# Gram products of the nodes divided between the first and the second layer's loop of the edge MLP

## The reference

```python
edge_index = jnp.stack([src, dst])
x = _layernorm(x + _L0_gnn_ref(src, dst, x, edge_attr_3, ...), axis=-1)   # attention on edges
x = _layernorm(x + _L1_gnn_ref(x, ..., edge_index), axis=-1)              # mean + batch norm
x = _layernorm(x + _L2_gnn_ref(x, src, dst, ...), axis=-1)
x = _layernorm(x + _L3_gnn_ref(x, edge_index, ...), axis=-1)

# in _L0_gnn_ref: an MLP on the three attributes of every edge
d = jax.nn.gelu(layer_norm(x @ Wd1 + bd1, g1, b1), approximate=False)
d = jax.nn.gelu(layer_norm(d @ Wd2 + bd2, g2, b2), approximate=False)
# in _L1_gnn_ref: statistics of h over all nodes
mu = jnp.mean(h, axis=0)
var = jnp.mean(jnp.square(h - mu), axis=0)
```

## Time and profile before

| | us |
|---|---|
| median of three timed runs | 4470.37 (4461.03 to 4475.22) |
| the profiled execution | 4428.03 |
| its span, first to last instruction | 4426.2 |
| GpSimd's scatter L482, first to last start | 162.2 to 485.4 |
| GpSimd's gather L497, first to last start | 489.9 to 786.7 |

### The profile page before, as it was taken

The page is one execution under the profiler, slowest core; times in us unless marked ns, Lnnn a source line. Parts: engine busy times, 40 slices in busy tenths (PEclk is TensorE's granted clock), DMA queues, the critical chain, the costliest instruction groups (busy, mean ns, idle before and its releaser), DMA issues. The chain is left out here.

```text
span 4426.2 us, 57341 instructions
## 1 busy us (share of the span) xinstructions
PE 2895.4 (65%) x14794; PEld 2110.8 (48%) x14794; DVE 2552.0 (58%) x4677; ACT 1648.0 (37%) x3762; POOL 2222.2 (50%) x2199
## 2 busy tenths in 40 slices
PE   0356782233433566998999999996879889942332
PEld 0255551122222455765666666664657655532221
DVE  3687741488888543454788877776633322233343
ACT  0233332133333000665788777871112133321111
POOL 0477777778777575001772000000057666567777
PEclk9976655566666666998999999996766699955555
DMA  3465302122222233566321111113455544422221
GB/s 106 121 153 133 89 0 60 43 61 65 59 58 61 65 79 70 121 132 136 85 62 59 57 57 57 57 49 70 92 122 147 140 126 126 114 67 50 51 56 33
DMA packets 879648, 364.12 MB, mean 82 GB/s; under 512 B 641845, under 2 KB 821447, under 8 KB 879570
## 3 DMA queue, kind: packets, MB, share of 16 engines
q1 hardware_dynamic: 815582, 335.56, 29.9%
q0 software_dynamic: 64000, 27.78, 3.3%
HBM read 237.51 MB, written 157.11 MB: 89 GB/s over the span
## 5 line engine op out<-in xcount | busy, mean ns | idle before, releaser
L1167 POOL DMA_INDIRECT g_W<-d,pos x400 | 422.0, 1055 | 1081.8 <-DMA g_W<-s 966.9
L859 POOL DMA_INDIRECT at_W<-in_x,at_idx x400 | 478.7, 1197 | 127.1 <-issue 125.4
L2788 POOL DMA_INDIRECT rows<-d,pos x200 | 212.0, 1060 | 408.8 <-DMA rows<-s 346.6
L919 PE MATMUL at_pA<-ident,at_W 128*128 128x128 f32 x200 | 55.7, 433 | 452.9 <-DMA at_W<-in_x,at_idx 413.0
L2641 PE MATMUL ou_pA<-ident,ou_W 128*128 128x128 f32 x200 | 55.1, 431 | 347.1 <-DMA ou_W<-d,pos 345.4
L482 POOL DMA_INDIRECT where<-mg_stage_v,mg_stage_i x200 | 243.2, 1216 | 71.2 <-issue 55.1
L919 PEld LDWEIGHTS at_pA<-ident,at_W 128*128 128x128 f32 x200 | 35.7, 216 | 466.0 <-DMA at_W<-in_x,at_idx 374.9
L1167 POOL DMA_INDIRECT me_W<-d,pos x200 | 207.6, 1038 | 99.3 <-issue 60.7
L1167 POOL DMA_INDIRECT ou_W<-d,pos x200 | 202.2, 1011 | 91.5 <-issue 60.7
L588 PE MATMUL mg_pG<-mg_z 128*128 128x129 f32 (+1 forms) x784 | 152.3, 372 | 142.2 <-DVE mg_z L729 142.2
L497 POOL DMA_INDIRECT mg_stage_v<-where,mg_stage_i x200 | 205.8, 1029 | 71.8 <-issue 55.0
(11 more groups left out here) (457 smaller groups left out, 8509.3 us busy)
## 6 DMA issues: line engine op xcount, KB each, us to landing
de_X<-x SPq DMA_DIRECT2D x98, 256.0 KB
out<-de_O SPq DMA_DIRECT2D x98, 256.0 KB, 2.2
mg_x<-in_x SPq DMA_DIRECT2D x97, 256.0 KB
x<-mg_z SPq DMA_DIRECT2D x97, 256.0 KB, 4.0
ix_win<-in_dstp SPq DMA_DIRECT2D x50, 256.5 KB, 3.2
at_V<-mlp SPq DMA_DIRECT2D x100, 128.0 KB
s<-g_HS SPq DMA_DIRECT2D x50, 256.0 KB
d<-g_HD SPq DMA_DIRECT2D x50, 256.0 KB, 2.3
```

Of the source, the lines that this page charges most:

```text
L859: gp.indirect_dma_start(out=W[w][b][:, (2 * t + h) * C:(2 * t + h + 1) * C], out_offset=None, in_=a["x"], in_offset=bass.IndirectOffsetOnAxis(
L919: i = t.transpose(pA[b][:, n * P:n * P + P], W[w][b][:, n * P:n * P + P], k.ident[:, :])
L1167: nc.gpsimd.indirect_dma_start(out=slot(w, b, t), out_offset=None, in_=table, in_offset=bass.IndirectOffsetOnAxis(ap=k.pos[:, c:c + 1], ax ...
L2788: nc.gpsimd.indirect_dma_start(out=k.rows[:, c * C:c * C + C], out_offset=None, in_=k.d2, in_offset=bass.IndirectOffsetOnAxis(ap=k.pos[:, ...
```

## The change

The first loop now has 25 iterations of one pair step and one edge part each, in which TensorE has the first layer ahead of the products of the pair before. The last iteration of it leaves one pair centred but not scaled. The third loop has, in each of its 25 iterations, the gelu part as before and one further pair step (the last one only finishes pair 48): 24 pairs are begun there. ScalarE now loads gelu's table set and the Ln and Exp set in turn, once each for an iteration. The loops of SP, ScalarE and VectorE that were loops of the hardware with registers as addresses are written out in the first and third loop. GpSimd's program and the second loop are not changed.

```diff
--- before.py
+++ after.py
@@ -446,7 +446,7 @@
         d = {n: g.sem("d_" + n) for n in ("sum", "cen", "sq", "sumsq", "ln", "dev", "norm", "gram")}
         pairs = D_FULL // 2 + 1
         ones_z = g.sem("ones_z")
-        assert D_FULL % 2 == 1 and pairs % 2 == 1 and pairs // 2 + 1 == ITERS
+        assert D_FULL % 2 == 1 and pairs % 2 == 1 and pairs == 2 * ITERS - 1
 
         def sizes(q):
             return (P, D_REST) if isinstance(q, int) and q == pairs - 1 else (P, P)
@@ -524,15 +524,15 @@
                         .then_inc(attr_in, 16)
                 load(0, 0)
                 load(1, 1)
-                with sp.Fori(0, pairs // 2 - 1) as j:
-                    load(2 * j + 2, 0)
-                    store(2 * j, 0)
-                    load(2 * j + 3, 1)
-                    store(2 * j + 1, 1)
-                load(pairs - 1, 0)
-                for q in range(pairs - 3, pairs):
-                    store(q, q % 2)
-                with sp.Fori(0, ITERS) as j:
+                for q in range(ITERS):
+                    load(q + 2, q % 2)
+                    if q:
+                        store(q - 1, 1 - q % 2)
+                for j in range(ITERS):
+                    q = ITERS + j
+                    if q + 2 < pairs:
+                        load(q + 2, q % 2)
+                    store(q - 1, 1 - q % 2)
                     for b in range(2):
                         sp.wait_ge(e["gelu", 2], last_of(j, b))
                         rows = k.mlp[:, bass.ds((2 * j + b) * CE, CE)].rearrange("c (n h e) -> c n h e", h=2, e=P)
@@ -589,15 +589,10 @@
                         i.then_inc(d["gram"], 1)
 
                 pe.wait_ge(attr_in, 64)
-                first_layer(0)
-                gram(0, 0)
-                for j in range(pairs // 2 - 1):
-                    gram(2 * j + 1, 1)
-                    first_layer(j + 1)
-                    gram(2 * j + 2, 0)
-                gram(pairs - 2, 1)
-                first_layer(ITERS - 1)
-                gram(pairs - 1, 0)
+                for j in range(ITERS):
+                    first_layer(j)
+                    if j:
+                        gram(j - 1, 1 - j % 2)
                 for b in range(2):
                     turn(0, b, 1)
                 with pe.Fori(0, ITERS - 1) as j:
@@ -607,9 +602,10 @@
                         turn(j + 1, b, 1)
                 for b in range(2):
                     second_layer(ITERS - 1, b)
-                with pe.Fori(0, ITERS) as j:
+                for j in range(ITERS):
                     for b in range(2):
                         turn(j, b, 2)
+                    gram(ITERS - 1 + j, j % 2)
 
             @block.scalar
             def _(act_):
@@ -654,15 +650,9 @@
                         square_edges(j, b, 1)
 
                 s.preload_act_table_set(LN_EXP)
-                deviate(0, 0)
-                squares(0)
-                with act_.Fori(0, pairs // 2 - 1) as j:
-                    deviate(2 * j + 1, 1)
-                    deviate(2 * j + 2, 0)
-                    squares(j + 1)
-                deviate(pairs - 2, 1)
-                deviate(pairs - 1, 0)
-                squares(ITERS - 1)
+                for j in range(ITERS):
+                    deviate(j, j % 2)
+                    squares(j)
                 deviations(1)
                 s.preload_act_table_set(GELU)
                 for b in range(2):
@@ -675,10 +665,13 @@
                 for b in range(2):
                     square_edges(ITERS - 1, b, 2)
                 deviations(2)
-                s.preload_act_table_set(GELU)
-                with act_.Fori(0, ITERS) as j:
+                for j in range(ITERS):
+                    s.preload_act_table_set(GELU)
                     for b in range(2):
                         gelu(j, b, 2)
+                    if ITERS + j < pairs:
+                        s.preload_act_table_set(LN_EXP)
+                        deviate(ITERS + j, (ITERS + j) % 2)
 
             @block.vector
             def _(dve):
@@ -740,18 +733,11 @@
                         v.memset(Z[w][b][:, :], 1.0).then_inc(ones_z, 1)
                 dve.wait_ge(ones_z, 4)
                 v.memset(attr[:, :], 1.0).then_inc(ones_in, 1)
-                step(0, None, 0)
-                center_edges(0, 1)
-                step(1, 0, 1)
-                sum_edges(0, 1)
-                with dve.Fori(0, pairs // 2 - 1) as j:
-                    step(2 * j + 2, 2 * j + 1, 0)
-                    center_edges(j + 1, 1)
-                    step(2 * j + 3, 2 * j + 2, 1)
-                    sum_edges(j + 1, 1)
-                step(pairs - 1, pairs - 2, 0)
-                center_edges(ITERS - 1, 1)
-                step(None, pairs - 1, 1)
+                for j in range(ITERS):
+                    step(j, j - 1 if j else None, j % 2)
+                    center_edges(j, 1)
+                    if j:
+                        sum_edges(j - 1, 1)
                 sum_edges(ITERS - 1, 1)
                 dve.wait_ge(dev, 1)
                 scale_edges(0, 1)
@@ -762,8 +748,11 @@
                 center_edges(ITERS - 1, 2)
                 sum_edges(ITERS - 1, 2)
                 dve.wait_ge(dev, 2)
-                with dve.Fori(0, ITERS) as j:
-                    scale_edges(j, 2)
+                scale_edges(0, 2)
+                for j in range(ITERS):
+                    step(ITERS + j if ITERS + j < pairs else None, ITERS + j - 1, (ITERS + j) % 2)
+                    if j + 1 < ITERS:
+                        scale_edges(j + 1, 2)
 
                 dve.wait_ge(d["gram"], 2 * pairs)
                 v.memset(k.gram[:, :], 0.0).then_inc(dev, 1)
```

## The result

The changed kernel takes 4491.5 us at the median of 19 runs, the kernel before 4461.0 us in 19 runs beside them: ratio 1.007, 95% interval 1.0043 to 1.0097, so it is slower by 0.7%, some 30 us. The forecast was 4475 us and "no change that can be told" as the likeliest case; the measured time lies inside the range of 4454 to 4500, but in another case than the likeliest, "slower by contention" (4497 us, chance 0.12). A second measurement on another chip gave 1.0065 (1.003 to 1.010).

What follows compares the result with a forecast made beforehand. GpSimd's list of 400 indirect DMAs was taken to bound the stage, hiding the other engines' 75 us gain. Pair steps +0.6 and landings +5 gave +5 us on the 4470.4 us median: 4475 us, range 4454 to 4500.

Steps and rivals of the forecast that it cites:

- no change that can be told: Whole kernel: likeliest case, 4475 us, within 0.3% (13.4 us), chance 0.71.
- slower by contention: Rival: each pair step moved to the third loop costs GpSimd the dear kind, +22 us, with landings +27; chance 0.12.
- the dear kind: A pair step whose VectorE groups cost GpSimd's DMAs about 1.95 us; upper bound for the 24 moved steps, +22 us.
- the -13: Lower bound for the 24 moved steps in us, if each costs GpSimd 0.5 us, the cheaper kind.
- a gather's mean over 1.2 us: Sign of being wrong: GpSimd's gather mean stays under 1.05 or passes 1.2 us; near 1.14 was expected.
- What bounds the stage: At the stage's end GpSimd's 400 indirect DMAs come last, some 36 us after everything the change touches.
- The first, second and third loop: First ends near 339 us, second takes 152, third runs from 492 to 680; the 75 us gain is hidden under GpSimd.
- Landings: GpSimd's waits for gathers beside third-loop node traffic: +6 us, less 1.0 at L492, so +5; ends 0 and +15.
- The cost of a step: GpSimd's DMAs lose 1.04 us per pair step, 26 us beside the scatter, 25 beside the gather, net +0.6 us.
- both kinds: Steps costing GpSimd about 1.95 or 0.5 us, expected by turns in the third loop too, hence 1.04 taken.
- Outlasting GpSimd: Rival: third loop takes 12.9 us an iteration and ends at 814 us, after GpSimd: 4494 us; chance 0.05.
- The free slip: Rival: third-loop VectorE groups stand apart, GpSimd slips in nearly free, -25 us, with landings -20: 4450 us; chance 0.10.

Runs made afterwards that it cites:

- e5: The changed kernel as it is, run again on another chip: 4477 us, ratio 1.0065.
- e6: The changed kernel with row sums and deviations of the pair steps in PSUM, run again on another chip: 4406 us, ratio 0.990.
- e7: The kernel before as it is, run with a trace on the second chip: 4467.8 us in one run.
- e9: The kernel before with its first loop written out on VectorE, ScalarE and SP, pair steps in the old order: 4422.5 us in one run.
- e3: The changed kernel with the deviations alone in PSUM, so only the centring has two SBUF inputs: 5129 us in one run on the first chip.
- e4: The changed kernel with the row sums alone in PSUM, so only the scaling has two SBUF inputs: 5175 us in one run on the first chip.
- e11: The changed kernel with two unused row sums of a constant on VectorE at the end of each first-loop iteration: 4486 us in one run.
- e12: The changed kernel with five unused row sums of a constant on VectorE at the end of each first-loop iteration: 4484 us in one run.
- e8: The changed kernel with VectorE's sum of squares between centring and scaling, and ScalarE's Exp waiting for the previous pair's scaling: 4421 us in one run.
- first four runs: e1 to e4, run on a chip on which the kernel before took 5087 us instead of 4461.
- e1: The changed kernel with row sums and deviations of the pair steps in PSUM, on the first chip: 5253 us.
- e2: The kernel before with row sums and deviations of the pair steps in PSUM, on the first chip: 5354 us.

## Why the prediction was right, and where it was not

**The number: in part luck.** The prediction added 5 us to a median of 4470.4 us from three runs. The kernel before took 4461.0 in 19 runs, and the change cost 30.5 us, six times the 5. Seen from 4470.4, the upper end of 4500 allowed 29.6 us. The range held because it took in the dear kind as a bound, and because its base was 9 us high. Its lower end, 4454, doesn't follow from the -13 named for it, which gives 4462. By its own sign, a gather's mean over 1.2 us, the prediction stands at the edge: 1.191 in the first trace, 1.211 in e5.

**What bounds the stage: right.** GpSimd came last by 36 us before and by 157 us after, and e6 shows it from the other side: 75 us less on its list, and the stage ended 74.6 us earlier, still with it.

**The first, second and third loop: right, and worth nothing, as said.** The third began at 483.7 us (492 said), took 7.2 us an iteration (7.5), and VectorE was done at 661 us (680 for the loop's end). The 48 more table loads, the unrolled programs and SP's longer queue stayed under GpSimd's list.

**Landings: over-sized.** 1.3 us more at the gathers' waits instead of 6, and 0.9 less ahead of L492, where 1.0 was said.

**The cost of a step: the term that was mis-sized.** "24 beside the gather, 25 us, at the same 1.04, since the third loop issues the same groups in the same order" took an average for a property of the instructions. It measured 1.56 us in the third loop, and 1.54 in the first, which the prediction costed as unchanged too: 26 us were said for its 25 steps, 38.4 came. The bounds were right (0.5 and 1.95), "both kinds will come by turns there too" was not.

The average was of two kinds of step. Add up the excess by pair in the traces of before, e7 and e9. Steps of even pairs stand behind the edges' sums (L702) and cost 1.54 to 1.58 us each: of 65 DMAs that met the two groups before their last instruction not one ran before the scaling's end. Steps of odd pairs stand behind the edges' centring (L694) and cost 0.53 to 0.60 us: all 47 DMAs held up there before the last instruction ran as soon as the VectorE instruction in progress ended, and 19 more, started in the same stretch, lost 0.1 us or nothing. Pairs 26 and 27 of the kernel before:

```profile
338.83 1.28 DVE L721 SCALAR_TENSOR_TENSOR mg_y<-mg_st,mg_x 128x512 f32<-128x512 f32 x2
...
339.59 2.57 POOL L482 DMA_INDIRECT where<-mg_stage_v,mg_stage_i  x1 [0.30 <-issue]
...
348.21 0.42 DVE L690 TENSOR_REDUCE mg_zs<-mg_pz 128x4 f32<-128x256 f32 x1 [1.28 <-PE mg_pz L557]
...
350.40 1.28 DVE L721 SCALAR_TENSOR_TENSOR mg_y<-mg_st,mg_x 128x512 f32<-128x512 f32 x2
...
351.17 1.36 POOL L482 DMA_INDIRECT where<-mg_stage_v,mg_stage_i  x1 [0.31 <-issue]
```

The DMAs start 0.76 and 0.77 us into the centring; one takes 2.57 us, the other 1.36. So it is not the start alone that decides. What differs is what VectorE did before. Ahead of the odd pair it had waited for TensorE's first layer (L690), 2.2 us before the centring, as ahead of all odd pairs from 3 on; ahead of the even one it had worked for 7.6 us without a wait. The waits of the kernel before, 165 to 500 us:

```profile
DVE mg_zs L690 <- PE mg_pz L557: 56.8, 44, 4.0
```

The changed kernel has the first layer ahead of the products, and VectorE waits 0.7 us in the same loop (170 to 330 us). This is what the change was meant to bring, and with it every step from pair 2 on is of the dear kind, 1.62 us on average, for even and odd pairs. The prediction named the wait's end, but not what it had to do with GpSimd. On the first chip, where VectorE did wait in the changed order, 10 DMAs in e3 and e4 were let in at the end of an instruction, all where the stretch with two SBUF inputs began 7 or 8 VectorE instructions after a wait, and 12 were held to its end, all where it began 21 or more after it. In e11 and e12, without waits, none was let in. The cause is thus narrowed down, but no run was made for it, and the third loop doesn't follow so plainly: there a wait of VectorE ends 3.05 us ahead of nearly every centring, and still 16 DMAs were held and only 4 let in.

e9 rules out that the written-out loop did it; e8 shows that the stretch of the two groups, not their number, sets the price; e6 removes the price altogether.

**The rivals.** Contention is what happened, at 1.55 us a step against the 1.39 from which it decides; its price had been put at 1.95 for the moved steps alone, and the real one lies between, for all 49. Outlasting GpSimd needed 12.5 us an iteration (790 + 13.4 less 492, over 25; the prediction says 12.8) and had 7.2. The free slip did not come: VectorE idled in loop three, but ahead of the sum of squares. The rule of the Trainium skill, page "SBUF — State Buffer", section "Who interferes with whom", held in its kinds: with one of the two inputs in PSUM the stall is gone (983 ns), which is its statement on instructions with at most one SBUF input. It gives the lock to one instruction ("for the whole instruction", said of the 2-port modes), and a DMA let in at that instruction's end is within it, other than the prediction has it: so it went in 5 cases of the changed kernel and 16 of the one before. That a DMA waits through up to three further instructions, 36 and 21 cases, is what it doesn't say.

**What stays open.** Why GpSimd gets in between VectorE's instructions soon after a wait of VectorE and not later, and why mostly not in the third loop; a run with a wait put ahead of the centring would test it. What slowed the first four runs' chip was not pursued; that TensorE's instructions came late there is seen, the reason is not.

## What to carry to other kernels

Where an engine that is not touched by a change comes last, ask what of its neighbours' work stretches it: an engine's time can be lost to its neighbour's instructions even when none of its own moves. A stall of two sequences that run side by side has no fixed price for a step, so an average from one arrangement must not be carried to another: split it by kinds of step first, and take the kinds as bounds. Here the waits that the rearrangement took from VectorE had stood ahead of just those steps that were cheap for GpSimd. Take the stall away before rearranging the rest: the row sums and deviations moved to PSUM gave 1% on two chips, the rearrangement alone cost 0.7%. On the first chip the same edit cost the kernel before 5.2%, so measure it on more than one.

## What the runs showed of the hardware

A GpSimd indirect DMA of 0.98 us (scatter) or 1.00 us (gather) takes up to 3.30 us in the changed kernel when it starts beside two VectorE groups with two SBUF inputs that stand back to back (2.5 us); held to the end, it ends 0.85 us (scatter) or 0.88 us (gather) after the last of them. In the first loop's odd steps of before, e7 and e9, 2.2 us after a wait of VectorE (pair 1: 3.7), the 47 that were held up ended 0.85 us (scatter) or 0.88 us (gather) after the instruction in progress instead. With the small operand in PSUM the same VectorE instructions last as long as before (a median of 0.680 us for the centring in e1 and 0.683 in e6 against 0.684 in the changed kernel), and GpSimd's longest scatter is 1.19 us. Two stretches of 1.28 us with 1.3 us between them cost 0.8 us a step, one of 2.5 us costs 1.55. And one chip ran the kernel before 14% longer (5087 us), e1's kernel 19% (5253 against 4406) and e2's 22% (5354 against 4394), with TensorE's instructions of a written-out loop up to 2.8 us apart in e1.
